# Small work re-ordered at the seams of the attentions, in the merged middle and in the last softmax of a fused transformer kernel

## The reference, cut to what matters

```python
x = x + L0_xattn(ln(x), ctx)   # 32 heads, 4 kv heads; keys are context and latents
x = x + L0_ffn(ln(x))          # dense product + 28 experts of rank 8, top 2
x = x + L1_xattn(ln(x), ctx)   # 32 heads, 8 kv heads, rms norm of q and k, mask
x = x + L1_ffn(ln(x))          # dense product + 8 experts of rank 8, top 2
x = x + L2_xattn(ln(x), ctx)   # linear attention: softmax of q over 8, of k over keys
x = x + L2_ffn(ln(x))          # 4 experts of rank 16, top 2, no dense product
x = x + L3_xattn(ln(x), ctx)   # one head of 512, rms norms of features, q and k
hits = softmax(ln(x) @ centroids.T / 0.1) > 0.01
row_sel = any(hits, tokens)[assignments]
x = x + where(any(hits, clusters) & row_sel, ln(x) @ weight.T + bias, 0)
```

## Time and profile before

| | us |
|---|---|
| median of 3 runs | 1504.78 (1501.4, 1504.78, 1504.82) |
| time of the profiled execution | 1501.78 |
| its span | 1500.1 |
| PE busy in it | 1462.8 |
| DVE, ACT, POOL busy | 1033.5, 927.2, 399.7 |

### The profile page before, as it was taken

One profiled execution on the slowest core, in us unless ns is written; L12 is line 12 of the kernel. 1 busy time (PEld: TensorE's weight loads), 2 busy tenths in 40 slices (PEclk: granted clock), 3 DMA queues, 4 the chain that ended last, 5 costly groups with the idle time before them and its releaser, 6 DMA issues.

```text
span 1500.1 us, 27932 instructions
## 1 busy us (share of the span) xinstructions
PE 1462.8 (98%) x9532; PEld 1307.5 (87%) x9532; DVE 1033.5 (69%) x2451; ACT 927.2 (62%) x3134; POOL 399.7 (27%) x458
## 2 busy tenths in 40 slices
PE   8999999999999999998999999999999999999997
PEld 7999999999999999886888888888888888887885
DVE  7556555665565557886677777777777778888776
ACT  4555445544564555546777777777777776377652
POOL 5112011201120112233233222232323232554431
PEclk9999999999999999999999999999999999999999
DMA  5100100010000100101020111111111101011101
GB/s 214 41 29 29 43 29 29 29 43 29 29 29 29 43 29 28 57 3 76 6 74 22 57 35 44 36 43 36 43 39 41 40 8 68 15 61 38 49 15 60
DMA packets 16116, 62.60 MB, mean 42 GB/s; under 512 B 2229, under 2 KB 3765, under 8 KB 10985
## 3 DMA queue, kind: packets, MB, share of 16 engines
q1 hardware_dynamic: 15976, 60.82, 11.7%
HBM read 58.72 MB, written 2.10 MB: 41 GB/s over the span
## 4 chain that ended last, share of the span: by engine, by line
PE 54%; issue 26%; DVE 9%; ACT 6%; POOL 4%; DMA 0%; SPq 0%; POOLq 0%; ACTq 0%; DVEq 0%
PE psY L957 12%; PE psQ L873 9%; PE psKV L897 7%; PE psSO L842 2%; PE psTP L858 2%; PE psSO L944 2%; POOL wo L541 2%; PE psQ L858 2%; PE psTP L907 2%; PE psQ L798 1%; PE psSO L843 1%; PE psTP L927 1%; ACT prob L1486 1%; PE psKV L813 1%; PE psQ L1244 1%
## 5 line engine op out<-in xcount | busy, mean ns | idle before, releaser
L957 PE MATMUL psY<-wo,oT 128*128 128x512 f32 x1536 | 378.0, 394 | 0.5
L957 PEld LDWEIGHTS psY<-wo,oT 128*128 128x128 f32 x1536 | 278.8, 188 | 55.6 <-POOL wo L541 2.2
L541 POOL TENSOR_TENSOR wo<-stage_o,wo 128x512 fp32r<-128x512 f32 x68 | 87.2, 1309 | 304.6 <-ACT wo L1399 279.5
L1399 ACT ACTIVATE pT<-psTP 64x256 fp32r<-64x256 f32 (+1 forms) x192 | 86.5, 451 | 126.5 <-PE psTP L927 125.8
L1489 ACT ACTIVATE prob<-wide,neg_mx 128x128 f32<-128x128 f32 x256 | 99.7, 390 | 78.8 <-DVE neg_mx L2081 78.8
L1949 DVE TENSOR_TENSOR pT<-psTP,pT 64x256 fp32r<-64x256 f32 (+1 forms) x192 | 97.8, 509 | 69.2 <-ACT pT L1399 67.4
L1486 ACT ACTIVATE prob<-s_sb,neg_mx 128x64 f32<-128x64 f32 x256 | 85.9, 337 | 94.3 <-DVE neg_mx L2081 94.3
L665 POOL TENSOR_TENSOR rms<-ms_eps,minus_half 128x5 f32<-128x5 f32 (+1 forms) x64 | 74.1, 1158 | 238.7 <-DVE ms_eps L2094 229.7
L541 POOL TENSOR_TENSOR wq<-stage_q,wq 128x512 fp32r<-128x512 f32 x42 | 53.6, 1293 | 210.8 <-ACT wq L1399 158.0
L897 PEld LDWEIGHTS psKV<-wkv,arena 128*128 128x128 f32 x768 | 100.3, 190 | 7.0 <-DVE kT L2129 1.9
L897 PE MATMUL psKV<-wkv,arena 128*128 128x256 f32 x768 | 102.6, 283 | 1.2 <-DVE kT L2129 1.2
(11 more groups left out here) (330 smaller groups left out, 3471.8 us busy)
## 6 DMA issues: line engine op xcount, KB each, us to landing
stage_o<-in_wo SPq DMA_DIRECT2D x16, 1024.0 KB, 4.8
stage_q<-in_wq SPq DMA_DIRECT2D x15, 1024.0 KB, 5.2
stage_kv<-in_wkv SPq DMA_DIRECT2D x12, 512.0 KB, 3.6
stage_q<-in_ctx SPq DMA_DIRECT2D x16, 256.0 KB, 3.1
stage_o<-in_ctxT SPq DMA_DIRECT2D x2, 1024.0 KB, 4.9
stage_q<-in_base SPq DMA_DIRECT2D x2, 1024.0 KB, 4.9
stage_kv<-in_ctx SPq DMA_DIRECT2D x8, 256.0 KB, 3.0
out<-x_res SPq DMA_DIRECT2D x8, 256.0 KB, 2.2
```

What stands on the lines that cost most here:

```text
L541: g.tensor_tensor(dst[LO], stage, dst[HI].bitcast(f32), ALU.subtract).then_inc(ld[done or what + "_lo"], 1)
L957: m = mm(psY[:], oT[:, ol, h, :], wo[:, wl, h, :], start=h == 0 and i == 0, stop=h == HQ - 1 and i == 2)
L1399: copy = lambda o, i: nc.scalar.activation(o, i, ACT.Copy)
```

## The change

It moves small instructions within the hand-written queues. On POOL: `ln_rstd(1, 3)` goes ahead of `low_wq(8)`; two of the four `wo` remainders go from the first two steps of attention 1 to behind `ln_rstd(2, 6)`; the wait on `prob` is left out at step 63; the product into `wide` comes from DVE to POOL at t = 7; the split of `wq3` is done two steps earlier. On ACT: four `wo` copies go from FFN steps 9 and 10 to step 8; at t = 1 of the middle the query's exponential goes first; `ln_norm_act(6, ...)` goes ahead of `k_squares`, the copies of `wq3` are done at t = 9 and 10. On DVE: the order in step 1 of attention 1, of `ln_lo(5, 4)` at t = 8, and of `keep` and the comparison at the end. On PE: FFN 2's hidden tile 3 goes to bank `psP` and waits for `y` (the value norm) in place of `experts_add`; `p_transpose` goes two products back. `assigned` and `selected` become f32r tiles in `wq`.

```diff
+    assigned, selected = wq[0:64, HI, 0], wq[0:64, HI, 1, 0:P]
     def hid_bank(f, n):
-        return psKV[:, 0:P] if n < 4 else psP[:, 0:P]
+        return psKV[:, 0:P] if n < 3 else psP[:, 0:P]
...
             ln_rstd(1, n)
-            if n == 2:
+            if n == 3:
                 low_wq(8)
...
             if n == 5:
                 low_wkv(10)
+            if n == 6:
+                low_wo(34, 2)
...
-            if t.exists and t.res(8) in (2, 3, 4, 5, 6, 7):
+            if t.exists and t.res(8) in (2, 3, 4, 5, 6, 7) and t.t < STEPS - 1:
                 pool.wait_ge(s["prob"], t.back(1).c + 1)
...
-            if t.t < 2:
-                for h in range(2 * t.t, 2 * t.t + 2):
+            if t.t == 0:
+                for h in range(2, KT):
                     low("wo", halves(wo, h), stage_o[:, h], wo_ready(t) + h + 1)
...
-            if t in (11, 12):
-                for k in range(2 * (t - 11), 2 * (t - 11) + 2):
+            if t == 7:
+                pool.wait_ge(ld["fn_in"], 32)
+                g.tensor_tensor(wide[:], stage_o[:, 0], stage_o[:, 1], ALU.mult).then_inc(N3["w"], 1)
+            if t in (9, 10):
+                for k in range(2 * (t - 9), 2 * (t - 9) + 2):
                     low("wq", halves(wq, k), stage_o[:, k], 72 + k + 1)
...
-            if f.index == 2 and n < 4:
+            if f.index == 2 and n < 3:
                 pe.wait_ge(s["x_add"], f.done + n)
...
-                if e == 5:
-                    pe.wait_ge(s["y"], NT)
+                if e in (4, 5):
+                    pe.wait_ge(s["y"], e + 3)
                 hidden_transpose(f, e - 1)
...
+                if t == NT + 1:
+                    pe.wait_ge(FS["hidT_lo"], f.done + 4)
                 value_product(t - 2)
...
-                    if k == 2 and b >= 0:
-                        p_transpose(b)
+                        if k == KT - 1 and i == 1 and b >= 0:
+                            p_transpose(b)
...
-            mm(psT[:], s_sb[0:64, 0:P], prob[0:64, :], start=True, stop=True).then_inc(C3["rows"], 1)
+            mm(psT[:], selected, assigned, start=True, stop=True).then_inc(C3["rows"], 1)
...
-            if t in (NT + 1, NT + 2):
+            if t == 8:
                 act.wait_ge(A["wo_used"], STEPS * 4)
-                for h in range(2 * (t - NT - 1), 2 * (t - NT)):
+                for h in range(KT):
                     high("wo", wo[:, HI, h], stage_o[:, h], 10 * 16)
...
             if t == 1:
-                hidden_hi(FF[1], NT - 1)
+                query_exp()
+                query_hi()
             if 1 <= t <= 4:
                 kvs_hi(t - 1)
+            if t == 1:
+                hidden_hi(FF[1], NT - 1)
...
-            if t in (10, 11):
-                act.wait_ge(ld["wo_in"], 20 * 16)
-                for k in range(2 * (t - 10), 2 * (t - 10) + 2):
-                    copy(wq[:, HI, k], stage_o[:, k]).then_inc(ld["wq_hi"], 1)
             if 0 <= e - 3 < NT:
                 ln_hi(6, e - 3)
+            if 0 <= e - 2 < NT:
+                ln_norm_act(6, e - 2)
+            if t in (9, 10):
+                act.wait_ge(ld["wo_in"], 20 * 16)
+                for k in range(3) if t == 9 else (3,):
+                    copy(wq[:, HI, k], stage_o[:, k]).then_inc(ld["wq_hi"], 1)
             if 0 <= n < NT:
                 k_squares(n)
-            if 0 <= e - 2 < NT:
-                ln_norm_act(6, e - 2)
...
                 if a.rms and t.t == 1:
                     row_max(t1)
+                    q_normalise(t)
                 if a.kv_new(t):
                     v_lo(t)
-                if a.rms and t.t == 2:
+                if a.rms and t.t in (1, 2):
                     k_normalise(t)
...
+            if t == NT:
+                ln_lo(5, t - 4)
             if 0 <= e - 1 < NT:
                 experts_add(f, e - 1)
-            if 0 <= t - 4 < NT:
+            if 0 <= t - 4 < NT and t != NT:
                 ln_lo(5, t - 4)
-            if t == 8:
-                dve.wait_ge(ld["fn_in"], 32)
-                V.tensor_tensor(wide[:], stage_o[:, 0], stage_o[:, 1], ALU.mult).then_inc(N3["w"], 1)
...
-                if p == NT + 1:
-                    keep(d - 1)
-                    dve.wait_ge(ld["asg_in"], 16)
-                    V.tensor_scalar(prob[0:64], q_sb[0:64].bitcast(i32), row_id[0:64], None, ALU.is_equal)
                 if 1 < c < NT:
                     ln_lo(next_ln, c)
+                if p == NT + 2:
+                    dve.wait_ge(ld["asg_in"], 16)
+                    V.tensor_scalar(assigned, q_sb[0:64].bitcast(i32), row_id[0:64], None, ALU.is_equal)
...
                     pT_lo(b)
+                if p == NT + 1:
+                    keep(d - 1)
```

More of the change, by code:

```diff
@@ L1784, in middle_step, with query_exp, query_hi @@
             s, f, e, n = M, FF[2], t - 5, t - 9
+            def query_exp():
+                act.wait_ge(s["nmr"], t)
+                need(act, s["q_lo"], t - 1)
+                nc.scalar.activation(q_sb[:], x[:, t - 1], ACT.Exp, bias=nmr[:, t - 1:t],
+                                     scale=rstd[:, t - 1:t]).then_inc(s["q_exp"], 1)
+            def query_hi():
+                act.wait_ge(s["q_exp"], t)
+                need(act, s["out"], t - 1)
+                copy(q_e[:, HI], q_sb[:]).then_inc(s["q_hi"], 1)
             if t < NT:
@@ L1804, in middle_step @@
                 gate_exp(f, e)
[L1805 to L1809, removed]
+            if 1 < t <= NT:
+                query_exp()
             if 0 <= t - 4 < NT:
@@ L2234, in attention @@
                     ln_lo(next_ln, t.t - LN_SLOT)
-                if t.exists and a.rms and t.t != 2:
+                if t.exists and a.rms and t.t not in (1, 2):
                     q_normalise(t)
@@ L2576, in clustered @@
             link(V.tensor_scalar(small[0:64, 0:1], psO[0:64, 0, 0:1], 0.5, None, ALU.is_ge))
-            V.tensor_scalar(s_sb[0:64, 0:P], ones[0:64].to_broadcast([64, P]), small[0:64, 0:1], None, ALU.mult).then_inc(s["sel"], 1)
+            V.tensor_scalar(selected, ones[0:64].to_broadcast([64, P]), small[0:64, 0:1], None, ALU.mult).then_inc(s["sel"], 1)
             dve.wait_ge(s["rows"], 1)
```

## The result

The changed kernel takes 1493.53 us in the median of five executions (1492.81 to 1495.88), the kernel before 1503.52 in the median of its five (1501.4 to 1504.82): ratio 0.9937, 95% interval 0.9926 to 0.9948. Forecast were 1497.7, faster, with a range of 1491.6 to 1502.5. Measured on both sides, the gain is 10.0 us; the sum of the prediction was 7.05. It was counted from the median of three executions, 1504.78, which five bring down to 1503.52.

What follows compares the result with a forecast made beforehand. PE was taken as the bound, working 1462.8 of 1500.1 us, with short waits left to remove. Ten gains summed to 7.05 us, taken from the 1504.78 median: 1497.7, range 1491.6 to 1502.5.

Steps and rivals of the forecast that it cites:

- rivals that leave little or nothing: Waits return on the same chain's next instruction, 1502.0 us, chance 0.15; or only the end of the kernel gains, 1503.4, 0.05.
- ten places: The ten spots in the kernel whose gains were forecast separately, together 7.05 us; lower ends give 1.7, upper ones 9.8.
- end of attention 1: POOL's `wkv` subtractions no longer wait for `prob`, so PE's wait for them goes: gain 0.65 us, ends 0 and 0.7.
- t = 1: Middle: with the query's exponential first on ACT, PE's wait for POOL's query remainder goes: 0.85 us, ends 0.3 and 0.85.
- last attend: DVE's `keep` and comparison go behind the remainder PE waits for: gain 0.7 us, ends 0.3 and 0.71.
- More goes than summed: Rival: no hold at attention 1's start and the middle freed to its upper ends, gain 9.2 us, 1495.6; chance 0.13.
- start of attention 1: PE's 2.07 us wait for the first `q_sb` goes, less 0.81 for POOL delaying `xn`: gain 1.3, ends 0.5 and 2.07.
- t = 8 and 9: Middle: hidden tile 3 in its own bank no longer waits for `x_res`: gain 0.65 us, ends 0 and 1.5.
- last softmax: Three waits of `p_transpose`, 0.8 us together, are covered by two more products: gain 0.6, ends 0.2 and 0.8.
- t = 9 to 12: Middle: POOL's earlier `wq3` subtractions stop holding DVE's `gate`, but the keys' chain bounds: gain 0.2 us, ends 0 and 0.7.
- Step 1: Attention 1: PE's 0.88 us wait for the second `q_sb` shrinks as `wo` remainders and `v_lo` move: 0.75, ends 0.4 and 0.88.
- Closing product: Kernel's end: one f32r product replaces two f32 instructions of 1.1 us together: gain 0.65 us, ends 0 and 0.7.

## Why the prediction was right, and where it was short

The direction and the mechanism came as worked out: PE's busy time stayed, its waits went, and neither of the rivals that leave little or nothing came. Seven of the ten places lie within their stated ends; the end of attention 1, t = 1 and the last attend lie above their upper ones (0.92, 1.20 and 0.86 against 0.7, 0.85 and 0.71). The time, 1493.53, lies inside the stated range but below the forecast's own 1495 to 1500, beyond the rival *More goes than summed* (1495.6) and not for that rival's reasons: POOL did hold `xn` at the start of attention 1, and t = 8 and 9 gave 0.56 of the 1.5 of their upper end. The sum was 1.4 us short on PE's starts and 3 on the medians, for three reasons.

- *"PE waits 0.7 for them ... Gain 0.65"* and the like at t = 1, at the last attend and for `p_transpose`: the step that priced a wait at its idle time. Where a wait vanished, more came back (0.92, 1.20 and 0.86 for 0.65, 0.85 and 0.7; at the transpositions of the last softmax 1.49 for 0.79 idle). The first three are 0.8 of the 1.4, the last softmax 0.2.
- *"I take 0.2, near the lower end for that chain"* at t = 9 to 12: 0.58 came, the other 0.4. The hold on `gate`, of which the price was known, went whole, and the keys' chain did not take it back; PE's three waits there (0.35, 0.33, 0.46) went, two for `oT` (0.31, 0.54) came. By the run with the norm put back, its place carries 0.1 to 0.3 of this.
- The clock was in no term. The two largest waits that went, for `q_sb` and `x_res`, are where the kernel before falls to 1.2 GHz in some executions, for 1.1 to 1.6 us each. That is of the size of the difference between 8.3 at equal clock and the 10.0 of the medians, though the clock of the executions behind that median of before is not on record; the profiled execution on which the sum rests had no such stretch, and the median from which it was counted, 1504.78, lies above all executions at 0.999 (1501.46 to 1502.19).

Of the rest: *start of attention 1* was right in kind and size (0.81 foreseen for POOL's hold; `xn` was 0.95 longer and PE lost 0.51 by it; 1.44 against 1.3). *Step 1* gave 0.63 for 0.75, but its reason was half right: the prediction added 0.74 for the pair of `wo` remainders and a tenth for DVE's order, where either alone would have done. *t = 8 and 9* gave 0.56 of the 0.65, the bank being the cause; `wide`, costed at nothing on POOL, does cost nothing there, while the same product on DVE at t = 7 would have cost 1.4. *Last softmax*, 0.80 for 0.6: 1.49 gained at four transpositions and 0.69 given back at two attends. At the first, 0.46, the remainder comes late behind `features`, as foreseen; at the other, 0.23, behind a stall of DVE that nobody foresaw (last section). *Closing product*, 0.69 for 0.65, one instruction of 0.49.

## What to carry to other kernels

Price a PE wait that vanishes at its idle time plus the overhang of the row ahead of it (0.16 or 0.25 here), and one that only shrinks at the idle time alone. Look for waits of which only the overhang is left to see (under 0.05 idle, 0.24 gained). Before taking two edits as a sum, ask whether they remove the same lateness: either alone may do. And where a kernel's executions spread by more than its edits are worth, compare executions of equal mean clock, or the starts of the same instruction in two traces.

## What the runs showed of the hardware that was not expected

The clock fell to its lower level behind waits of PE of only 0.6 to 2.2 us, in some executions and not in others of the same kernel (above). And there is a small stall of DVE's own: at the seventh tile's `pT` DVE stands 0.27 us idle though its input, ACT's `pT`, was done at 1464.65.

```profile
1465.11 0.29 DVE L1967 TENSOR_TENSOR pT<-psSO,pT 128x128 fp32r<-128x128 f32 x1 [0.27 <-DVE small L2502]
```

The DMA queues of the same trace from 1464 to 1466 us (packets, MB, share of 16 engines) have one packet of instructions there:

```profile
q14 instruction: 1, 0.01, 1.1%
```

All eight traces in which DVE has one instruction fewer, `wide` being on POOL, show 0.26 to 0.27 at this instruction; the five with `wide` on DVE show at most 0.04. PE's `attend` behind it waits 0.18 for `pT`, and the run with `wide` on DVE at t = 7, which lacks the stall, gains 0.22 there against the changed kernel. That an instruction load is what DVE waits for was not tested.
